# Repeated products of constants in front of the transposes of five stages and of one pass over exponentials

## The reference

```python
x = x + L0_xattn(ln(x), ctx, mask)          # attention over 8192 context rows
x = x + L0_attn(ln(x))                      # rotary attention; it normalises its own input again
x = x + L0_ffn(ln(x))
x = x + L1_xattn(ln(x), ctx)
x = x + L1_attn(ln(x))                      # out @ Wu.T + bu
x = x + L1_ffn(ln(x))                       # h + shared_mlp(h) + 16 experts, two per token by a sigmoid gate
x = x + L2_xattn(ctx, ln(x))                # softmax(h @ ctx.T) @ ctx
x = x + L2_attn(ln(x))                      # rms norm, causal attention
x = x + L2_ffn(ln(x))
x = x + L3_xattn(ln(x), ctx, ctx)
x = x + L3_attn(ln(x))                      # out @ Wout + bout
x = x + L3_ffn(ln(x))                       # two inner layers: local attention, then a gated MLP
```

## Time and profile before

| | |
|---|---|
| median of 3 runs | 2098.92 us (2096.85 to 2101.7) |
| the profiled execution's own time | 2092.45 us |
| its span in the profile | 2091.1 us |
| mean granted TensorE clock | 0.958 of full speed |
| PE busy | 1898.7 us, 91% of the span |
| DVE, ACT, POOL busy | 65%, 58%, 26% |

### The profile page before, as it was taken

How to read it: one execution, slowest core, us unless ns; L and a number is a source line. 1 busy time by engine, 2 the same in 40 slices (tenths; PEclk the granted TensorE clock), 3 DMA queues, 4 the chain that set the end, 5 groups by cost and what they waited for, 6 DMA issues and landing times.

```text
span 2091.1 us, 36908 instructions
## 1 busy us (share of the span) xinstructions
PE 1898.7 (91%) x13679; PEld 1191.1 (57%) x13679; DVE 1357.4 (65%) x3230; ACT 1219.4 (58%) x2766; POOL 543.0 (26%) x697
## 2 busy tenths in 40 slices
PE   7999999988998899999999778898898799798998
PEld 4555555544565355555555557657556688564656
DVE  4676667874767577667787476631356898477373
ACT  3787778886444278777889452342155687164251
POOL 2211111112630211011100265200033466254151
PEclk9999999999999799999999888999999899999999
DMA  9677667751112767757762213333101242200110
GB/s 207 152 143 138 127 123 144 146 106 40 41 42 50 127 116 147 133 121 151 145 91 32 83 33 108 109 103 101 46 21 57 86 123 71 86 1 9 41 54 11
DMA packets 114226, 191.48 MB, mean 92 GB/s; under 512 B 17096, under 2 KB 67073, under 8 KB 107521
## 3 DMA queue, kind: packets, MB, share of 16 engines
q1 hardware_dynamic: 113056, 188.11, 40.9%
q10 hardware_dynamic: 992, 1.02, 0.2%
HBM read 135.20 MB, written 2.69 MB: 66 GB/s over the span
## 4 chain that ended last, share of the span: by engine, by line
PE 67%; DVE 19%; ACT 5%; DMA 3%; SPq 3%; issue 3%; POOL 1%; ACTq 0%; DVEq 0%; POOLq 0%
PE PS L795 9%; PE PS L687 8%; DVE WK L858 7%; PE PS L357 6%; PE PS L704 5%; PE PS L675 5%; PE PS L365 5%; PE PS L716 4%; PE PS L1877 3%; PE PS L1902 3%; PE PS L466 2%; PE PS L2252 2%; PE PS L2310 2%; PE PS L493 2%; PE PS L514 2%
## 5 line engine op out<-in xcount | busy, mean ns | idle before, releaser
L858 DVE TENSOR_REDUCE WK<-PS 128x1 f32<-128x1024 f32 x512 | 623.1, 1223 | 241.8 <-PE PS L687 166.1
L966 ACT ACTIVATE WK<-PS 128x512 f32<-128x512 f32 x840 | 464.1, 600 | 42.7 <-PE PS L687 20.9
L687 PE MATMUL PS<-QSR,KSR 51*128 51x256 f32 x2048 | 379.7, 307 | 20.1 <-DVE WK L858 13.1
L687 PEld LDWEIGHTS PS<-QSR,KSR 51*128 51x128 f32 x2048 | 251.4, 187 | 255.4 <-ACT WK L966 90.6
L675 PE MATMUL PS<-KSR,QSR 51*128 51x512 f32 x1024 | 371.3, 454 | 8.7 <-DMA QSR<-scratch_q 3.4
L795 PE MATMUL PS<-WK 128*32 128x256 f32 x2528 | 220.3, 394 | 7.2 <-ACT WK L950 7.2
L675 PEld LDWEIGHTS PS<-KSR,QSR 51*128 51x128 f32 x1024 | 186.3, 188 | 20.8 <-issue 12.7
L565 ACT ACTIVATE WK<-PS,WK 128x256 f32<-128x256 f32 (+1 forms) x320 | 140.6, 451 | 74.5 <-DVE WK L533 45.4
L1042 POOL TENSOR_SCALAR nbw<-WK 128x4 fp32r<-128x4 f32 x64 | 12.7, 198 | 576.0 <-DVE WK L864 575.9
L989 POOL TENSOR_TENSOR WK<-WK 128x512 fp32r<-128x512 f32 x62 | 79.2, 1278 | 232.6 <-ACT WK L927 125.3
L591 POOL TENSOR_TENSOR WK<-WK 128x128 f32<-128x128 f32 (+1 forms) x128 | 64.9, 507 | 254.4 <-DVE WK L551 218.9
(11 more groups left out here) (358 smaller groups left out, 3534.0 us busy)
## 6 DMA issues: line engine op xcount, KB each, us to landing
KSR<-WK SPq DMA_DIRECT2D x381, 128.0 KB
WB<-in_ctxT SPq DMA_DIRECT2D x78, 512.0 KB, 5.1
WK<-in_ctxT SPq DMA_DIRECT2D x40, 512.0 KB, 4.1
WA<-in_ctxT SPq DMA_DIRECT2D x26, 512.0 KB, 5.2
WK<-in_ctx SPq DMA_DIRECT2D x8, 1024.0 KB, 6.1
WK<-in_ctx SPq DMA_DIRECT2D x16, 512.0 KB, 4.3
QSR<-scratch_q SPq DMA_DIRECT2D x48, 128.0 KB, 4.4
WB<-in_L3f_qkv SPq DMA_DIRECT2D x2, 1536.0 KB, 6.4
```

What stands on the lines that cost most here:

```text
L687: return pe.e.matmul(tile["S", L, s, i][:, j * 256:j * 256 + 256], KS[s % 4][HALF[i % 2], kt * 128:(kt + 1) * 128], QS[HALF[i % 2], g % 2, ...
L858: dv.e.tensor_reduce(mt[:, n:n + 1], tile["R", L, s, n].rearrange("p a b -> p (a b)"), AX, ALU.max).then_inc(*dv.at("R", L, s, n))
L966: ac.e.activation(PR[n % NPR], tile["S", L, s, i], ACT.Exp).then_inc(*ac.at("E", L, s, i))
```

## The change

A new helper issues `n` products of the constant bf16 identity `idb` (128 x 128) with a constant bf16 mask `msk` (128 x 512) into the PSUM bank that the next transposes will fill. Nothing reads them: the transposes overwrite the bank. `turn_pe` gets a parameter for it, and six places use it: 18 products in `l0a`, 26 in `l1f`, 12 in `l2x`, 22 in `l2a`, 18 in the first inner layer of `l3f`, each behind `after` and `settle` and ahead of the first transpose, and 18 in `l2x` ahead of the first transposes of exponentials (`bb == 0`, `g == 0`, `q == 0`). That is 114 products. Of DVE's mark `msk` the wait is long fulfilled: `after` has already waited for later marks.

```diff
+        def keep_warm(b, n):
+
+            pe.wait_ge(dv, "msk")
+            for i in range(n):
+                pe.e.matmul(b.ap, idb[:, :], msk[:, 0, :], start=True, stop=True)
+
-        def turn_pe(tag, src, of, *by):
+        def turn_pe(tag, src, of, *by, warm=0):
 
             for f in range(2):
                 b = take(banks, (tag, f), (by[f], tag, f))
                 settle(b)
+                if f == 0 and warm:
+                    keep_warm(b, warm)
                 for t in range(NT):
...
-            turn_pe("h0", XR, (dv, "ln0b"), dv, ac)
+            turn_pe("h0", XR, (dv, "ln0b"), dv, ac, warm=18)
...
-            turn_pe("h1f", XN, (dv, "ln1f"), dv, ac)
+            turn_pe("h1f", XN, (dv, "ln1f"), dv, ac, warm=26)
...
-            turn_pe("h2x", XN, (dv, "ln2x"), dv, ac)
+            turn_pe("h2x", XN, (dv, "ln2x"), dv, ac, warm=12)
...
                             b = take(ring, ("p2", n), ((dv, ac)[q], "p2", n))
                             settle(b)
+                            if bb == 0 and g == 0 and q == 0:
+                                keep_warm(b, 18)
                             pe.wait_ge(ac, "e2", bb, q)
...
-            turn_pe("h2a", XR, (dv, "rms2"), dv, dv)
+            turn_pe("h2a", XR, (dv, "rms2"), dv, dv, warm=22)
...
-            turn_pe(("hs", l), XN, (dv, "xl", l), dv, ac)
+            turn_pe(("hs", l), XN, (dv, "xl", l), dv, ac, warm=18 if l == 0 else 0)
```

## The result

The changed kernel takes 2109.05 us (median of 22 runs, 2100.94 to 2118.65) against 2097.81 us for the kernel before (median of 22, 2088.29 to 2111.75). The ratio is 1.0046, 95% interval 1.0028 to 1.0063: slower by 0.46%, which is 9.6 us (5.9 to 13.2). The forecast was 2108 us, from a term sum of +9.0. The profiled execution took 2102.96 us with a span of 2101.7, which is 10.6 us more than the span of before.

What follows compares the result with a forecast made beforehand. PE, busy 91% of the span, was taken as the bound, its half clock mattering only where others wait for it. Six terms sum to +9.0 us; added to the median of 2098.92 they give 2107.9, rounded to 2108 us, range 2100 to 2115.

Steps and rivals of the forecast that it cites:

- The price of a product: One added product on PE takes 0.22 us at full clock, 0.43 at half, with its load of weights hidden.
- `l0a` -0.8: Into `l0a`, 18 products: transposes 1.0 us late, 1.76 back in the records behind; -0.8 us, ends -2.5 and +0.4.
- `l1f` +5.2: Into `l1f`, 26 products: 5.2 us late, all arriving at the experts through DVE's chain; ends +4.9 and +6.4.
- `l2x` +0.7: Into `l2x`, 12 products: 2.4 us late, 1.65 back in the scores; +0.7 us, ends -0.9 and +1.5.
- exponentials +3.9: Exponentials in `l2x`, 18 products: no wait to fill, no clock to save; +3.9 us, ends 3.8 and 4.3.
- `l2a` -0.3: Into `l2a`, 22 products: hidden, clock falls again ahead of L357, only faster transposes count; -0.3 us, upper end +0.5.
- `l3f` +0.3: Into `l3f`, 18 products: 3.0 us late, 2.7 back in L365; +0.3 us, ends 0.0 and +1.5.
- it holds: Case not chosen for `l2a`: the clock stays full into L357, saving its 2.8 us at half clock as well; -1.7 us.
- the clock holds from the first product on: Rival: clock holds at joints starting near full, is back at once elsewhere; sum +1.0 us, 2099.9 us; chance 0.12.
- The 3.4 chosen for c: In runs begun at half clock, the clock returns after 3.4 us, adding 1.67 us; the four stretches gave 2.8 to 5.4.
- products of constants don't bring it back: Rival: each added product costs 0.43 us in half clock and transposes their 2 us; +30 us, 2129 us; chance 0.05.
- the products fill the wait: Rival: products fill the idle time from its start, nothing late, clock never falls; -6.2 us, 2092.7 us; chance 0.05.

Runs made afterwards that it cites:

- the kernel with the other four places: Changed kernel without the products into `l1f` and at the exponentials; `l0a` 18, `l2x` 12, `l2a` 22, `l3f` 18 stay: 2093.99 us, ratio 0.9996 to the kernel before.
- `l1f` alone: Changed kernel with only the 26 products into `l1f` kept: 2103.48 us, ratio 1.0026 to the kernel before.
- the exponentials alone: Changed kernel with only the 18 products ahead of the first transposes of exponentials kept: 2101.05 us, ratio 1.0024 to the kernel before.
- `l1f`, 52 products: Products in `l1f` alone, 52 instead of 26; one execution, 2108.5 us.
- the early placing: Changed kernel with the joints' products issued ahead of `after`, those at the exponentials put at batch 1: 2087.86 us, ratio 0.9959 to the kernel before.
- the three later kernels with early products: Early products in larger numbers, 0.9969; also four behind the joints' transposes, 0.9968; also weights for `l2a` loaded after the context columns, 0.9946; ratios to the kernel before.

## Why the prediction was right

**The price of a product** held. At full clock the 18 products in the chain take 3.88 us, 0.216 each; at half clock, in the kernel with the other four places, twelve take 5.28 us to the end of the last, 0.43 from start to start. Loads were hidden: beside 3.80 us of uninterrupted products at 1405.40 PEld is busy 1.78 us, 0.10 for each of 18, and no time stands between them. The Trainium skill, "TensorE: Matmul & The Clock Gate", section "LDWEIGHTS (loading the stationary operand)", gives 0.107 us for such a load, and the trace agrees with its 0.10; the 12 us that it would have cost unhidden did not come.

**The joints.** Forecast and profile: `l0a` -0.8 and -0.98; `l1f` +5.2 and +5.25; `l2x` +0.7 and +0.54; exponentials +3.9 and +3.88; `l2a` -0.3 and -1.7; `l3f` +0.3 and +0.37. The sum was +9.0; measured in the joints it is +7.4, and the ratio gives +9.6. The mechanism held place by place, above all at the two that carry the sum. That the total came within 1 us is partly luck: the interval of the ratio alone is 7.3 us wide.

**The term that was mis-sized** is `l2a`. The prediction chose "it falls again just ahead of L357" over "it holds"; in the changed kernel it held, and gave the -1.7 stated for that case (L365's 64 records take 27.70 us instead of 29.11). In the kernel with the other four places it fell, as forecast. Both are outcomes of the same code, and I can't say what decides between them; no run here separates it. The -1.7 itself hangs on the one profile of before: with `l1f` alone and with the exponentials alone, where nothing is changed in `l2a`, the same distance is 1.6 us longer than in it, because the half-clock stretch there lasts 13.7 us instead of 10.2.

**What the sum left out**, and named among what could make it fail, is the clock elsewhere. From within the first dense products of `l2a` (L357, now L365) to the mark of `l3f`, 4.2 us were lost in instructions that are the same in both kernels (windows of before, then of after; the clock stands before the last two columns):

```profile
1503.00:1883.70 380.70, 330.61 (x2074) 248.37 (x2072) 272.63 (x1562) 217.44 (x664) 167.96 (x201) 0.96 0.20 61
```

```profile
1509.10:1894.00 384.90, 334.62 (x2074) 250.03 (x2073) 272.84 (x1563) 217.32 (x664) 168.29 (x202) 0.95 0.19 60
```

It is this, less 0.5 in the experts and 0.8 in the rest of `l2x`, that takes the +7.4 to the +10.6 of the spans. Nothing ties it to the change: the same stretch changed by -1.8, -3.1 and -0.7 us in the three kernels with a part of the change, and with the products placed early by -1.8 in the first and +4.2 in the last. The single places timed over many runs agree with the terms (+5.5 and +5.0 us for `l1f` and the exponentials, nothing measurable for the other four), within intervals that are as wide as the terms.

**The rivals.** That the clock holds from the first product on (2099.9) is refuted at four joints, where it came back between 3.1 and 3.7 us after the first product (into `l0a` at 504.5, products from 501.29; into `l1f` at 1248.6, products from 1244.95), and right at `l2a` alone. The 3.4 chosen for c lies in the middle of these, with some luck: other profiles give 3.3 (`l1f`, 52 products), 4.0 (`l1f` alone; `l3f` with the other four) and 6.0 us (`l2x` there), the last outside the 2.8 to 5.8 that the ends were worked out with. That products of constants don't bring it back (2129) is refuted by the windows. The Trainium skill says on the same page, in "What's actually happening", that throttled is the default and activity releases it: the trace agrees, with this delay. That the products fill the wait (2092.7) is refuted for this code, by the 7.40 us of idle time ahead of them, and shown for the other placing. There its mechanism was half right: nothing is late, but "the clock never falls" failed, since it fell again behind the products at five places and held at all five joints only when there were more products and four of them stood behind the transposes as well.

## What to carry to other kernels

Filler work can pay only where the engine would really stand idle: ahead of the wait, not behind it, and never at a place where the chain of waits already runs through that engine. So before placing it, read in the timeline who ends the idle time (here DVE's mark) and whether the next stage waits for this engine or for a chain on another (the gate of `l1f`, where a full clock gives nothing back). And look at what follows a removed stall: here the clock fell again in the next gap, and with a half-clock stretch moved from a gap onto dense work a place can lose (`l2a`, +1.3); then transfers of weights that nobody needed yet held up a load that the scores needed at once.

## What the runs showed of the hardware that was not expected

The same program scatters by 18 us, and the clock explains most of it. Over the 22 runs of the changed kernel the mean granted clock lies between 0.955 and 0.965, the fastest run (2100.94 us) at 0.965 and the slowest (2118.65 us) at 0.955; time and clock correlate with -0.90, at 16.7 us for each 0.01. An 0.01 of mean clock is 0.02 of the span at half, some 42 us, so each microsecond at half clock costs about 0.4 us, near the 0.5 that the prediction used for dense work. Where half-clock stretches fall inside unchanged, dense stages differs from program to program (0.96 against 0.98 in the stretch of 4106 records above, 7.7 us), and from run to run. The 7.7 us are not fixed to the early placing: in the profiles of the three later kernels with early products the same instructions changed by -4.4, +0.6 and -1.4 us. Whether the placing has any share in them stays open. One profile can't tell a change of this size from that. The distances between marks within a joint tell more, though not everywhere: with nothing changed at the place itself, `l1f` and the scores stay within 0.03 us, but `l3f` moves by 0.8 and `l2a` by 1.6.
